# Half rows by column residue: a new frame for x1 and x2, and the focal input and modulation stages rewritten on it

## What is computed

```python
# layer 0
x = x + window_attention(ln(x))           # shifted 7x7 windows, shift 3, 4 heads
x = x + top2_of_8_experts(ln(x))
# layer 1
x = x + focal_modulation(ln(x))
x = x + recurrence(ln(x))                 # y_t = sigmoid(bn(W x_t) + V y_(t-1)) over 3136 pixels

def focal_modulation(x):                  # B, H, W, C
    y = x @ Wf + bf                       # C -> 2C + 4
    q, ctx, gates = y[..., :C], y[..., C:2*C], y[..., 2*C:]
    ctx_all = 0
    for l, k in enumerate((k0, k1, k2)):  # depthwise 3x3, 5x5, 7x7
        ctx = gelu(dwconv_same(ctx, k))
        ctx_all += ctx * gates[..., l:l+1]
    ctx_all += gelu(mean(ctx, axis=(1, 2))) * gates[..., 3:]
    out = q * (ctx_all @ Wh + bh)
    out = (out - mean(out)) * rsqrt(var(out) + 1e-3) * gamma + beta
    return out @ Wp + bp
```

## Time and profile before

| | |
|---|---|
| median of 3 runs | 10527.13 us (10521.58 to 10538.14) |
| the profiled execution | 10524.25 us, its span 10522.5 us |
| TensorE, weight loads | 8609.7 us busy (82%), 5525.2 us (53%) |
| VectorE | 6874.4 us (65%) |
| ScalarE | 5282.8 us (50%) |
| GpSimd | 5917.0 us (56%) |
| DMA | 961.46 MB, 36.8% of 16 engines' span |
| granted TensorE clock, mean | 0.945 of full speed |

### The profile page before, as it was taken

The page is one execution under the profiler, slowest core; times in us unless marked ns, Lnnn a source line. Parts: engine busy times, 40 slices in busy tenths (PEclk is TensorE's granted clock), DMA queues, the critical chain, the costliest instruction groups (busy, mean ns, idle before and its releaser), DMA issues. The chain is left out here.

```text
span 10522.5 us, 333676 instructions
## 1 busy us (share of the span) xinstructions
PE 8609.7 (82%) x109757; PEld 5525.2 (53%) x109757; DVE 6874.4 (65%) x22569; ACT 5282.8 (50%) x14181; POOL 5917.0 (56%) x7369
## 2 busy tenths in 40 slices
PE   7888888878888888677759999995666668888888
PEld 5666666633333333355535555555666655555554
DVE  7888888878888888777725555556778772222222
ACT  4555555545555555566634444444666653333333
POOL 7777777767777777666612222224555554444444
PEclk9999999989999999888879999997888889999999
DMA  1111111111111111498943444437888862222222
GB/s 48 49 49 49 49 49 50 50 48 50 50 48 47 50 50 46 93 178 177 177 135 156 161 158 158 158 129 127 145 142 144 137 110 54 56 56 56 56 56 54
DMA packets 1199080, 961.46 MB, mean 91 GB/s; under 512 B 338169, under 2 KB 1078457, under 8 KB 1190202
## 3 DMA queue, kind: packets, MB, share of 16 engines
q1 hardware_dynamic: 1198522, 956.38, 36.8%
HBM read 576.97 MB, written 455.45 MB: 98 GB/s over the span
## 5 line engine op out<-in xcount | busy, mean ns | idle before, releaser
L943 PE MATMUL moe_pe_out<-moe_we,moe_xnT 128*128 128x512 f32 x3136 | 1531.6, 623 | 373.0 <-DVE moe_odd L836 197.2
L1533 PE MATMUL conv_pc<-conv_c,conv_toep 128*128 128x432 f32 (+1 forms) x3584 | 1370.5, 535 | 0.0
L740 ACT ACTIVATE moe_scaled<-moe_pe_out,moe_gate 128x128 f32<-128x128 f32 x3136 | 891.9, 367 | 867.6 <-PE moe_pe_out L943 865.8
L2092 ACT ACTIVATE rec_yT<-rec_ph 128x32 f32<-128x32 f32 x3136 | 618.5, 197 | 1241.7 <-PE rec_ph L2213 1241.7
L1384 POOL TENSOR_TENSOR conv_g<-conv_c,conv_gate 128x896 f32<-128x896 f32 x128 | 365.1, 2852 | 1462.9 <-DVE conv_out L1496 1362.8
L943 PEld LDWEIGHTS moe_pe_out<-moe_we,moe_xnT 128*128 128x128 f32 x3136 | 557.3, 195 | 1188.3 <-issue 1187.2
L2213 PE MATMUL rec_ph<-rec_yT,rec_vt 128*32 128x32 f32 x25080 | 843.1, 207 | 196.5 <-ACT rec_yT L2092 121.7
L1533 PEld LDWEIGHTS conv_pc<-conv_c,conv_toep 128*128 128x128 f32 x3584 | 672.1, 190 | 599.1 <-issue 599.1
L2139 DVE COPY rec_xT<-rec_pin 128x512 f32<-128x512 f32 x196 | 135.6, 692 | 1240.9 <-PE rec_pin L2185 1240.9
L281 POOL TENSOR_SCALAR att_xn<-att_xin,att_mv,att_rstd 128x128 f32<-128x128 f32 x1024 | 868.2, 857 | 54.1 <-POOL att_rstd L277 54.1
L678 POOL TENSOR_TENSOR moe_paired<-moe_scaled 128x256 f32<-128x256 f32 x784 | 569.3, 726 | 537.2 <-ACT moe_scaled L740 521.5
(11 more groups left out here) (194 smaller groups left out, 21904.3 us busy)
## 6 DMA issues: line engine op xcount, KB each, us to landing
conv_toep<-rows_dram SPq DMA_DIRECT2D x32, 2304.0 KB, 12.6
c<-foc_cs SPq DMA_DIRECT2D x32, 1856.0 KB, 12.0
conv_cin<-c SPq DMA_DIRECT2D x32, 1856.0 KB, 7.5
x<-att_x1s SPq DMA_DIRECT2D x3584, 14.0 KB
ctx_all<-conv_out SPq DMA_DIRECT2D x32, 1792.0 KB, 5.7
att_xin<-x_windows SPq DMA_DIRECT2D x512, 98.0 KB
moe_xin<-x SPq DMA_DIRECT2D x112, 448.0 KB, 3.5
x<-moe_acc SPq DMA_DIRECT2D x112, 448.0 KB, 2.7
```

The costliest lines, as they stand in the source:

```text
L740: ins = act.activation(scaled[:, b, e, :], pe_out[:, b, 1, e * C:(e + 1) * C], ACT.Identity, scale=g)
L943: ins = pe.matmul(pe_out[:, b, half, :], xnT[:, n.slot(2), t, :], we[:, half * 4:half * 4 + 4, :].rearrange("d e c -> d (e c)"), start=Tru ...
L1533: ins = pe.matmul(pc[k][:, half, 0:HALF * wide].rearrange("p (b i) -> p b i", i=wide)[:, :, i0:i1], w, tile[:, n.slot(slots), b, i0 + away ...
L2092: act.activation(yT[:, a, cs], ph[:, a, cs], ACT.Sigmoid).then_inc(moved, 1)
```

## The change

x1 and x2 no longer lie in pixel order but in a frame: per image 2 x 56 half rows (112 partitions) of 28 columns each, the columns of the shifted image sorted by their remainder modulo 7, so that a window's columns fall in the same places in each row. Attention then stores a step in 4 DMAs instead of 14, with the same 392 runs of 512 B. Focal input and modulation load an image in 4 DMAs with runs of 14336 B.

Focal input: biases enter through the last row of the weights (channel 127 of the normed tile is 1, and the last row of Wf is subtracted from the others); POOL norms two tiles of four and ScalarE two; VectorE spreads the transposed tiles into a picture in true pixel order (xnT, 58 rows of 64); the query is computed transposed (weights stationary, 8 picture rows moving) and stored as q[C, pixels]; context and gates are computed from two picture rows at a time and copied out by ScalarE, context now with the tile innermost (c0: P, B, C, ODD). Steps are 7 an image, 224 in all, norms 9 ahead, statistics 11 ahead.

Convolution: cin is loaded with the channel outside of the tile, in runs of 464 B, and TensorE reads it without the copy.

Modulation: the modulator is transposed too (one product of 448 columns), VectorE adds bh and multiplies with q in one operation, in three pieces, and lays the result out by tiles of the frame (yT); ScalarE squares it. The projection comes before the norm: wpx is gamma Wp with each column's mean taken off, its last column 1/C gives the mean of y, a second product the mean of its square; the residual multiplies the projected tile with the inverse root. One pow of 8 numbers makes both roots. x3 is stored in pixel order in 17 DMAs an image.

```diff
@@ attention, SP
-                    for r1 in range(WS):
-                        p0 = odd * 64 + r1 * WS
-                        sp.dma_start(dram(x1, n.val(WS * IMG * C, (r1 * IMG + odd * WS) * C),
-                                          [(C, WS), (2 * WS * C, PAIRS), (1, C)]),
-                                     x1s[p0:p0 + WS, n.slot(4), :, :]).then_inc(x1_out[n.slot(4)], 16)
+                    for part in range(2):
+                        at = part * IMG * 28 * C + n.off % 8 * WTOK * 4 * C + odd * C
+                        sp.dma_start(dram(x1, Step(n.loop, 1, n.off // 8).val(PIX * C, at),
+                                          [(4 * C, WTOK), (2 * C, 2), (1, C)]),
+                                     x1s[odd * 64:odd * 64 + WTOK, n.slot(4), 2 * part:2 * part + 2, :])\
+                          .then_inc(x1_out[n.slot(4)], 16)
@@ new loads
+def load_quads(eng, dst, src, n, sem):
+    for half in range(2):
+        for row, real, rows in ((IMG - SHIFT, 0, SHIFT), (0, SHIFT, IMG - SHIFT)):
+            p0 = half * IMG + real
+            eng.dma_start(dst[p0:p0 + rows, :, :].rearrange("p k c -> p (k c)"),
+                          dram(src, n.val(PIX * C, (half * IMG + row) * TILES * C), [(TILES * C, rows), (1, TILES * C)]))\
+               .then_inc(sem, 16)
@@ focal input, SP
+                if c == 0 and last < -2 * NG:
+                    hold(sp, normed, n.val(1, NG), ticks)
+                    hold(sp, normed_act, n.val(1, NG), ticks)
+                    load_quads(sp, xin[:, s, :, :], x2, m + 2, x_in[s])
+                if c < NG - 1:
+                    return
+                hold(sp, q_read, n.val(1, 1), ticks)
+                sp.dma_start(dram(q, m.val(PIX), [(B * PIX, C), (1, PIX)]), qs[:, s, :]).then_inc(q_out[s], 16)
+                hold(sp, c_read, m.val(NG + 1, NG + 1), ticks)
+                sp.dma_start(dram(c0, m.val(C * ODD), [(B * C * ODD, P), (1, C * ODD)]),
+                             cs[:, s, :, :, :].rearrange("p c j -> p (c j)")).then_inc(c_out[s], 16)
+                hold(sp, g_read, m.val(NG + 1, NG + 1), ticks)
@@ focal input, POOL
+                hold(pool, nmean_done, n.val(1, 1), ticks)
+                for t in range(HERE):
+                    ins = pool.tensor_scalar(xn[:, n.slot(2), t, 0:C - 1], xin[:, m.slot(2), GRP * c + t, 0:C - 1],
+                                             rstd[:, a, t:t + 1], nmean[:, a, t:t + 1], ALU.mult, ALU.add)
+                if last < -10:
+                    scale(n + 10)
+                if last < -9:
+                    norm(n + 9, first + 9)
@@ focal input, ACT
+                for i, j, jn in pair_groups(c):
+                    hold(act, c_made, m.val(NG + 1, i + 1), ticks)
+                    act.activation(cs[:, s, :, j:j + jn].rearrange("p c j -> p j c"), py[:, i % 2, 0:jn, 0:C], ACT.Copy)\
+                       .then_inc(c_read, 1)
@@ focal input, DVE
+                for h0, hn, k0, kn, at in quad_columns(c):
+                    at += h0 * EVEN + k0 * WS
+                    last_col = at + (hn - 1) * EVEN + (kn - 1) * WS
+                    to = xnT[:, s, 1:1 + IMG, at:last_col + 1:WS] if last_col > at else xnT[:, s, 1:1 + IMG, at:at + 1]
+                    ins = dve.tensor_copy(to.rearrange("p r (h k) -> p h k r", h=hn), rows[:, h0:h0 + hn, k0:k0 + kn, :])
+                ins.then_inc(xT_out, 1)
+                if last < -11:
+                    layer_stats(n + 11, first + 11)
+                if last < -9:
+                    negate(n + 9, first + 9)
+                if last < -8:
+                    spread(n + 8, first + 8)
@@ convolution
-                act.activation(cch[:, n.slot(4), :, :], cin[:, g.slot(2), :, :, n.off % PER], ACT.Copy).then_inc(spread_out, 1)
+                sp.dma_start(cin[:, s, :, :, :].rearrange("p b c j -> p b (c j)"),
+                             dram(c0, g.val(PER * ODD), [(B * C * ODD, P), (C * ODD, B), (1, PER * ODD)]))\
@@ modulation, POOL
+                if first >= 3:
+                    hold(pool, z_normed, n.val(1, -2), ticks)
+                hold(pool, varied, n.val(1, 1), ticks)
+                pool.tensor_tensor(rstd[:, n.slot(2), :], var[:, n.slot(2), :], halfneg[0:TOK, :], ALU.pow).then_inc(rstd_done, 1)
+                if last < -2:
+                    add_bias(n + 2)
+                roots(n + 1, first + 1)
@@ modulation, DVE
+                for h, a, wide in ((0, 0, EVEN), (1, 0, EVEN - SHIFT), (1, EVEN - SHIFT, SHIFT)):
+                    real = (h * EVEN + a + SHIFT) % IMG
+                    ins = dve.scalar_tensor_tensor(out=yT[:, s, a:a + wide, h, rows].rearrange("p a r -> p r a"),
+                                                   in0=mod[:, :, real:real + wide], scalar=hcol[:, 0:1],
+                                                   in1=qry[:, :, real:real + wide], op0=ALU.add, op1=ALU.mult)
+                if last < -9:
+                    gate(n + 9, first + 9)
+                if first >= 1:
+                    negate(n - 1, first - 1)
+                residual(n)
+                if last < -1:
+                    y_mean(n + 1)
+                x_parts(n)
+                if last < -1:
+                    y_mean_square(n + 1)
+                x_statistics(n)
+                if last < -1:
+                    y_variance(n + 1)
+                x_variance(n)
@@ modulation, PE
+                for t in range(GRP):
+                    pe.matmul(pz[0:TOK, b, t, 0:C + 1], tile_of(yT, m, c, t), wpx[:], start=True, stop=True)
+                    ins = pe.matmul(pz[0:TOK, b, t, C + 1:C + 2], tile_of(sq, m, c, t), mean[:, 0:1], start=True, stop=True)
```

More of the change, by code:

```diff
@@ L973, with quad_columns, focal_input_stage @@
 G_ALL = sum(G_LEN)
[L976 to L984, removed]
-    for half in range(2):
[L987 to L995, removed]
+TILES = 28
+GRP = 4
+PART = 2 * IMG
+def load_quads(eng, dst, src, n, sem):
+    for half in range(2):
+        for row, real, rows in ((IMG - SHIFT, 0, SHIFT), (0, SHIFT, IMG - SHIFT)):
[3 more added lines that the diff above has]
+               .then_inc(sem, 16)
+def quad_columns(g):
+    at = g + SHIFT
+    if at < WS:
+        return [(0, 2, 0, 4, at)]
+    return [(0, 1, 0, 4, at), (1, 1, 0, 3, at), (1, 1, 3, 1, at - IMG)]
+def focal_input_stage(nc, B, x2, Wf, bf, ident, q, c0, gates):
     EPS = 1e-6
     OUT = 2 * C + 4
[L1003 to L1009, removed]
+    NG = TILES // GRP
+    N = B * NG
+    U = 2 * NG
+    AHEAD = 14
+    HERE = 2
+    ROWS8 = IMG // NG
     S = Stage(nc, "foc")
@@ new lines, in norm, with query @@
+                for t in range(HERE, GRP):
+                    ins = act.activation(xn[:, n.slot(2), t, 0:C - 1], xin[:, m.slot(2), GRP * c + t, 0:C - 1], ACT.Identity,
+                                         bias=nmean[:, a, t:t + 1], scale=rstd[:, a, t:t + 1])
+                ins.then_inc(normed_act, 1)
+            def query(n, first):
+                m, c = image(n)
+                if c == 0 and first >= 2 * NG:
+                    hold(act, q_out[m.slot(2)], m.turn(2, 16), ticks)
+                hold(act, q_made, n.val(1, 1), ticks)
+                at = c * ROWS8 * IMG
+                act.activation(qs[:, m.slot(2), at:at + ROWS8 * IMG], pq[:, n.slot(2), 0:ROWS8 * IMG], ACT.Copy).then_inc(q_read, 1)
@@ L1166, in step @@
-                for y, t, tn, up, value in pairs(n):
-                    act.wait_ge(gates_read, value)
-                    act.activation(qs[:, m.slot(2), t:t + tn, :], py[:, y, 0:tn, 0:C], ACT.Copy).then_inc(q_read, up)
+                    for k in range(9):
+                        norm(n + k, k)
+                query(n, first)
+                if last < -9:
+                    norm(n + 9, first + 9)
+                context(n, first)
             run_steps(act, N, U, step, AHEAD)
@@ L1238, in turn, with query @@
                 ins.then_inc(turned, 1)
+            def query(n, first):
+                m, c = image(n)
+                if c == 0:
+                    hold(pe, xT_out, m.val(NG, NG), ticks)
+                if first >= 2:
+                    hold(pe, q_read, n.val(1, -1), ticks)
+                pe.matmul(pq[:, n.slot(2), 0:ROWS8 * IMG].rearrange("p (r w) -> p r w", w=IMG), wf[:, 0:C],
+                          xnT[:, m.slot(2), 1 + c * ROWS8:1 + (c + 1) * ROWS8, 0:IMG], start=True, stop=True).then_inc(q_made, 1)
@@ new lines, in context @@
+            def context(n, first):
+                m, c = image(n)
+                for i, j0, jn in pair_groups(c):
+                    if first >= 2 or i >= 2:
+                        hold(pe, c_read, m.val(NG + 1, i - 1), ticks)
+                        hold(pe, g_read, m.val(NG + 1, i - 1), ticks)
+                    for j in range(jn):
+                        r = 2 * (j0 + j)
+                        ins = pe.matmul(py[:, i % 2, j, 0:C + 4], xnT[:, m.slot(2), r:r + 2, :].rearrange("p r w -> p (r w)"),
```

(8 more changed lines are left out.)

663 lines of the change are left out of this document (291 added, 372 removed).

## The result

The changed kernel takes 13006.7 us (median of 4 runs, 13001.9 to 13010.4) against 10530.7 for the kernel before beside it: ratio 1.235, 95% interval 1.233 to 1.237. Forecast were 10065 us. The change makes the kernel 2476 us slower, and not through any of the rivals.

A forecast was written before the change was run, and what follows sets the result against it. Bounds: attention the DMA queue, convolution TensorE, focal input and modulation rings of waits. Attention -300, focal input -110, convolution 0, modulation -50 make -460 us, from 10522.5 to 10062, said as 10065; range 9900 to 10230 for 8 in 10.

The forecast's parts named there:

- E: Focal input: the moment when the last context of an image is copied, from which the landing of x is counted.
- the one on the slower side: Focal input: the context's scattered copy on ScalarE at 9 ns an element makes the kernel slower, 10760 us; chance 0.05.
- forecast -300: Attention: 14 stores become 4, the queue stops bounding, and VectorE's 6.95 us a step replaces 8.19.
- Rival 3: Attention: a DMA costs by its bytes or runs, the queue stays at 7 us or more, total 10365; chance 0.08.
- forecast 25.6 us an image and -110 us: Focal input: 28.7 us an image falls to 25.6, POOL's seven 3.2 us steps plus a 3.3 us stall for x.
- Rival 1's first half: Focal input: x arrives in time and POOL's pace is reached, -214 us, total 9960; whole rival's chance 0.15.
- forecast 6.2 us a step: Modulation: a step falls from 6.42 to 6.2 us, -50 us over 224 steps.
- The meeting of negation and bias sum: Modulation: VectorE's negation is held until POOL's 1.27 us bias sum ends, so residuals begin again at 6.0 us.
- the lower bound: Modulation: -250 us if the negation isn't held, at 5.0 us a step.
- its cover is 2 us: Modulation: VectorE's gate, three pieces and 0.9 us, lies in the wait for POOL's root and costs nothing.
- Scattered writes, taken at 1.1 to 2 ns and free: Focal input's context and spread, modulation's gate: writing each 4-byte element to its own line, 1.1 to 2 ns, costs nothing.
- rivals 2 and 4: Scattered writes cost 4 ns, 10175 up to 10230, chance 0.18; context's scattered copy at 9 ns, 10760, chance 0.05.

The follow-up runs named there:

- attention alone: The kernel before with the changed attention stage only, later stages reading misplaced values at unchanged work: 10212.8 us, ratio 0.971.
- 48 + 5 kernel: The changed kernel with each load of 53 rows cut into one of 48 and one of 5: 10291.8 us, ratio 0.979 to before.
- the early load: 48 + 5 kernel with focal input's load of x issued two steps earlier, ahead of the three stores: 9913.6 us, ratio 0.944.
- the free negation: 48 + 5 kernel with GpSimd waiting for VectorE's negation before adding the bias in the modulation: 10159.7 us.
- 49 + 4: The changed kernel with each load of 53 rows cut into one of 49 and one of 4: 10399.9 us.
- 47 + 6: The changed kernel with each load of 53 rows cut into one of 47 and one of 6: 12704.9 us.

## Why the prediction was wrong

The step that failed is one clause of the focal input's: "some 4 us more, and 1 to 3 us for pieces of 3 and 53 rows that don't divide by 16 engines. It lands at E + 13 to 15." I saw that the piece doesn't divide by 16 and priced it as a remainder, as if 53 rows were handed out to 16 engines in four rounds. They go to one engine: the two long loads take 57 us, and the focal input is 47 us an image longer for them (1515 / 32). The modulation takes the same load and got no such term at all: only the loads of context were priced there (30 us of lead, 13 needed). No rival had it either; the one on the slower side was put on ScalarE. The rows of before have no transfer with a prime number of rows over 16 (attention's stores have 7). But two things spoke against the change, and I drew on neither: the Trainium skill's rule, cited above, and the kernel before itself. Its loads of x meet a run of 53 too, of columns, and cut it into 5 and 48. The new frame has the run in its rows and gave up that cut (each triple is first column, first place and number):

```python
COLS = ((53, 0, 3), (0, 3, 5), (5, 8, 48))
```

The sum by spans: from before to the changed kernel +2479.3 us (10522.5 to 13001.8). It is made of

- attention -311.7 (forecast -300): right, in cause and size. The queue was the bound, the number of DMAs its price, and VectorE's 6.96 us came next. Rival 3 is out. (The prediction's "784 runs" a step are 392; at 2 ns a run this makes its argument stronger.)
- the prime piece +2712.2 (forecast: within 1 to 3 us an image in the focal input, some 60): 1515 us in the focal input, 1201 in the modulation, less 4 between runs of different kernels.
- the rest of the change +78.8 (forecast -160), read between attention alone and the 48 + 5 kernel: focal input to the first product of the convolution +52.6 (5083.5 to 5136.1), convolution to the modulation's first statistics of x +17.5, modulation's steps +7.4, the end +1.3.

*Focal input, forecast 25.6 us an image and -110 us.* Measured with 48 + 5 rows: 30.5 us an image. Against attention alone the copies take 37 us longer (960.6 against 923.6), the start 24 us longer and the end 9 us less, together the +52.6. The mechanism was right, x late behind the stores in one wait an image, but the term was 3.3 us and measured 11.2. It was mis-sized at both ends. The landing is at E + 18.6, not E + 14: the six issues take 4.3 us and the last lands 11 us behind its issue. And VectorE wants x at E + 7.4, not E + 10.6, because the step is 2.4 to 2.7 us and not 3.2: GpSimd's half of the norm, priced from a row of another form (0.82 us), takes 0.46, in the changed kernel as with 48 + 5 rows:

```profile
L1106 POOL TENSOR_SCALAR foc_xn<-foc_xin,foc_rstd,foc_nmean 112x127 f32<-112x127 f32 x448 | 202.5, 462 | 1886.2 <-DVE foc_nmean L1198 1884.4
```

So the landing sets the image: 18.6 us from E to x, and some 12 from there to the next E. The start failed too: x lands no sooner (first statistics at 4039.7 us, with attention alone at 4038.1), where 11 us were taken, and from there to the first copy the deeper pipeline takes 36.7 us against 14.1, where +10 were taken. Rival 1's first half (x in time) would have been 22.3 us an image; the early load shows 18.6.

*Convolution, forecast 0, bounds -5 and +15.* Measured +11.8 from its first to its last product; the other 5.7 of the +17.5 lie between that and the modulation's first statistics. The products straight out of cin take 547 ns on the median and those out of the copy 539, which for 1024 of them would be some 8 us; it was not tried.

*Modulation, forecast 6.2 us a step.* Measured 6.46. The meeting of negation and bias sum is real (0.9 us, and the free negation brings the step to 5.70, not to the 5.0 of the lower bound; that bound doesn't fit its own sum, as 5.0 us a step would be 318 us and not 250). The step that failed is that of the gate, which "lies in that wait and costs nothing; its cover is 2 us": the gate was covered as work on VectorE, but what it waits for was not followed. The modulator stands behind a projection that needs a residual of the same ring; that costs 0.4 us a step.

*Scattered writes, taken at 1.1 to 2 ns and free.* Measured 2.1 ns an element on ScalarE (1072 ns for 512), and free there; VectorE's two were not tried side by side. The choice of the nearest row was right, rivals 2 and 4 are out.

## What to carry to other kernels

Look at the size of the outermost dimension of every DMA that a new layout creates, before anything else: a frame that is neat for the engines can leave a transfer with a prime number of rows over 16, and that piece ran at one engine's pace here. When the old code cuts a load oddly (5 and 48 places), ask what for before you drop it. When a stage turns slow while all engines and the DMA share fall, read the GB/s slices: a flat line at a sixteenth of the peak was such a transfer here, and cutting it into a multiple of 16 and a rest mended it. Then ask for every load how many steps lie between the moment its buffer is free and its place in the queue, and for every operation that is hidden, what it waits for, not only how long it is.

## What the runs showed of the hardware that was not expected

- One DMA engine moved 53 rows of 14336 B at 22 to 29 GB/s, 0.54 us a row; all of them together up to 452 GB/s in the same window. Against 48 + 5 rows, 49 + 4 cost the kernel 108 us more and 47 + 6 cost it 2413.
- GpSimd's norm as multiply and add takes 462 ns for 112 x 127 elements; the nearest row before, subtract and multiply on 128 x 127, took 821. Which of the differences makes it was not tried.
- A copy from PSUM on ScalarE that writes each 4-byte element 116 B apart takes 1072 ns for 512 elements, side by side 574.
- The same small negation takes 159 ns alone and up to 0.99 us beside GpSimd's bias sum:

```profile
7520.94 1.27 POOL L1705 TENSOR_TENSOR mod_xin<-mod_xin,mod_brow 112x512 f32<-112x512 f32 x1
...
7521.24 0.99 DVE L1851 SCALAR_TENSOR_TENSOR mod_nmean<-mod_mv,mod_rstd 112x4 f32<-112x4 f32 x1
```
